# Attention output projection with its weights held in the array, and two edits at the kernel's ends

## What is computed

```
x = x + attention(layernorm(x)) @ Wo      # 16 heads, key width 8, value width 64, causal
x = x + moe(layernorm(x))                 # 8 experts, each takes its top 64 of 256 tokens per batch
                                          # gelu(xin @ w1) @ w2, hidden 512, scaled by the gate's probability
```

## Time and profile before

| | us |
|---|---|
| median of 3 runs | 532.89 |
| the profiled execution | 532.7 |
| its span | 531.0 |
| TensorE busy in the span | 511.3 |
| VectorE, ScalarE, GpSimd busy | 421.9, 397.4, 262.8 |

### The profile page before, as it was taken

The page is one execution under the profiler, slowest core; times in us unless marked ns, Lnnn a source line. Parts: engine busy times, 40 slices in busy tenths (PEclk is TensorE's granted clock), DMA queues, the critical chain, the costliest instruction groups (busy, mean ns, idle before and its releaser), DMA issues.

```text
span 531.0 us, 13930 instructions
## 1 busy us (share of the span) xinstructions
PE 511.3 (96%) x4783; PEld 424.6 (80%) x4783; DVE 421.9 (79%) x1080; ACT 397.4 (75%) x1380; POOL 262.8 (49%) x252
## 2 busy tenths in 40 slices
PE   3799999999999999999999999999999999999996
PEld 2477787787887787787787787877889998999996
DVE  6778889888898898889999999998874677634444
ACT  4799998989889898998989889898654544434330
POOL 8955656556655655656555655665633110011121
PEclk9889999999999999999999999999999999999999
DMA  6575234551622505234151331503200012000002
GB/s 184 174 188 159 79 82 134 185 159 59 183 97 62 158 7 151 79 79 137 24 160 60 102 112 49 160 0 82 81 1 1 2 39 63 22 12 21 11 22 61
DMA packets 48583, 45.70 MB, mean 86 GB/s; under 512 B 3344, under 2 KB 45328, under 8 KB 48528
## 3 DMA queue, kind: packets, MB, share of 16 engines
q1 hardware_dynamic: 47696, 44.33, 28.9%
q10 hardware_dynamic: 832, 0.66, 0.4%
HBM read 26.09 MB, written 18.89 MB: 85 GB/s over the span
## 4 chain that ended last, share of the span: by engine, by line
PE 92%; DVE 2%; ACT 2%; issue 2%; DMA 1%; POOLq 0%; POOL 0%; ACTq 0%
PE ctx_ps L1272 17%; PE misc_ps L1281 11%; PE t_ps L1359 10%; PE t_ps L1245 6%; PE t_ps L1246 5%; PE t_ps L1255 5%; PE misc_ps L1183 4%; PE s_ps L1343 4%; PE misc_ps L1185 4%; PE s_ps L1231 3%; PE misc_ps L1184 3%; PE s_ps L1344 3%; PE s_ps L1345 3%; PE s_ps L1218 3%; PE s_ps L1227 3%; PE ctx_ps L1369 2%
## 5 line engine op out<-in xcount | busy, mean ns | idle before, releaser
L587 ACT ACTIVATE prob<-s_ps,neg_max 128x128 f32<-128x128 f32 (+1 forms) x512 | 209.9, 443 | 0.6 <-DVE neg_max L1100 0.3
L511 POOL TENSOR_TENSOR probn<-prob,inv 128x1024 f32<-128x1024 f32 x64 | 121.2, 1893 | 34.1 <-DVE inv L1080 33.8
L587 ACT ACTIVATION_READ_ACCUMULATOR prob<-s_ps,neg_max 128x1 f32 x512 | 118.1, 231 | 0.0
L504 POOL TENSOR_TENSOR probn<-prob,inv 128x512 f32<-128x512 f32 x64 | 66.6, 1040 | 74.8 <-PE t_ps L1255 74.1
L635 ACT ACTIVATE hT<-s_ps 128x512 f32<-128x512 f32 x64 | 37.9, 597 | 63.4 <-PE s_ps L1345 60.9
L1016 DVE TENSOR_REDUCE neg_max<-s_ps 128x4 f32<-128x1024 f32 x63 | 76.5, 1214 | 5.7 <-PE s_ps L1231 3.5
L1281 PE MATMUL misc_ps<-wo_sb,ctxT 128*128 128x128 f32 x512 | 67.7, 275 | 0.0
L540 POOL TENSOR_TENSOR y_parts<-y_sb,y_parts 128x512 fp32r<-128x512 f32 x16 | 21.2, 1328 | 93.9 <-ACT y_parts L645 93.9
L1281 PEld LDWEIGHTS misc_ps<-wo_sb,ctxT 128*128 128x128 f32 x512 | 62.2, 192 | 0.2 <-issue 0.2
L1245 PE MATMUL t_ps<-ident,probn 128*128 128x128 f32 x256 | 61.7, 281 | 0.0
L1246 PE MATMUL t_ps<-ident,probn 128*128 128x128 f32 x256 | 60.1, 275 | 0.0
(11 more groups left out here) (199 smaller groups left out, 1175.9 us busy)
## 6 DMA issues: line engine op xcount, KB each, us to landing
qT<-q_rows SPq DMA_DIRECT2D x14, 512.0 KB, 4.1
q_rows<-qk_hi SPq DMA_DIRECT2D x16, 256.0 KB, 2.2
q_rows<-qk_lo SPq DMA_DIRECT2D x16, 256.0 KB, 2.7
k_rows<-qk_hi SPq DMA_DIRECT2D x15, 256.0 KB, 2.6
k_rows<-qk_lo SPq DMA_DIRECT2D x15, 256.0 KB, 2.8
k_diag_even<-k_rows SPq DMA_DIRECT2D x28, 128.0 KB, 4.4
k_diag_odd<-k_rows SPq DMA_DIRECT2D x28, 128.0 KB, 4.5
w_raw<-in_L_ffn_w SPq DMA_DIRECT2D x1, 2048.0 KB, 9.3
```

What stands on the lines that cost most here:

```text
L504: nc.gpsimd.tensor_tensor(probn[r][:, 0:HG * P].rearrange("p (i k) -> p i k", i=HG), prob[r][:, 0:HG * P].rearrange("p (i k) -> p i k", i=HG),
L511: nc.gpsimd.tensor_tensor(probn[r][:, HG * P:].rearrange("p (i k) -> p i k", i=HG), prob[r][:, HG * P:].rearrange("p (i k) -> p i k", i=HG ...
L587: last = nc.scalar.activation(prob[r][:, first + i * keys:first + (i + 1) * keys], scores[:, i, :], ACT.Exp, bias=neg_max[:, r, block_, i: ...
```

## The change

Three groups of edits:

**Projection.** In batches 0 to 14 a chunk of Wo (128 x 128) is the stationary operand and the context chunk moves with all its 256 tokens: 2 matmuls a unit. The sum of a batch comes out with tokens along the free axis. ScalarE copies it to `xn2` at the end of unit j = 2 of the next batch (`copy_sums`), TensorE turns it back with two transposes after the contexts of j = 3 (`turn_sums`) into the other half of `misc_ps[1]`, and `add_x` reads it there. Batch 15 keeps the old form.

**Start.** The own keys are made before the own queries, in separate PSUM banks; ScalarE makes the keys' signed copy and writes two of the four key blocks, VectorE the rest by copies. The stores of batch 0 are split: group 1 first (SyncE and ScalarE), the rest on SyncE. GpSimd waits for `own_ready` before wv_lo. Values of unit 1 go to `misc_ps[1]`, so that the values of unit 2 need no copy to be done first; ScalarE's copies of both move from unit 0 to unit 1.

**End.** VectorE makes both parts of the last expert product's result itself (`last_y`, 1 + 4 instructions). TensorE finishes batches 12, 13 and 14 one after the other, and batch 15 in two halves of 128 tokens in banks of their own. VectorE adds these in tiles, and the stores are issued one by one, by SyncE (12, 14, the last half) and ScalarE (13, the first half).

```diff
+        last_halves = [to[:, 0:T].rearrange("p (a d) -> p a d", a=2) for to in (misc_ps[1], s1_ps[:, 0, :])]
...
-        own_ps = misc_ps[1][:, :].rearrange("p (w t) -> p w t", w=2)
+        own_ps = [misc_ps[1][:, 0:T], t_ps[0][:, 0:T]]
...
+                if b == 0:
+                    group, rest = slice(HG, 2 * HG), slice(2 * HG, H)
+                    store_rows(sp, b, qk_hi, K_HI, group, group_stored)
+                    sp.wait_ge(qk_lo_done, b + 1)
+                    store_rows(sp, b, qk_lo, K_LO, group, group_stored)
+                    for source, rows in ((qk_hi, Q_HI), (qk_hi, K_HI), (qk_lo, Q_LO), (qk_lo, K_LO)):
+                        store_rows(sp, b, source, rows, rest)
+                    sp.wait_ge(group_stored, QK_STORES)
+                    sp.wait_ge(zeroed[b], 1)
+                    load_rows(b, slice(1, 2), group_loaded)
+                else:
+                    store_rows(sp, b, qk_hi, Q_HI)
                     store_rows(sp, b, qk_hi, K_HI)
-                sp.wait_ge(qk_lo_done, b + 1)
-                store_rows(sp, b, qk_lo, Q_LO)
-                if b > 0:
+                    sp.wait_ge(qk_lo_done, b + 1)
+                    store_rows(sp, b, qk_lo, Q_LO)
                     store_rows(sp, b, qk_lo, K_LO)
                 sp.wait_ge(qk_stored, QK_STORES * (b + 1))
...
+            for b in range(LAST, B - 1, 2):
+                sp.wait_ge(out_ready, b + 1)
+                sp.dma_start(out_tiles[:, b * TB:(b + 1) * TB, :], x_all[:, b * TB:(b + 1) * TB, :]).then_inc(stored, 16)
+            sp.wait_ge(last_half_ready, 2)
+            sp.dma_start(out_tiles[:, B * TB - 1:, :], x_all[:, B * TB - 1:, :]).then_inc(stored, 16)
+            sp.wait_ge(stored, 16 * (B + 1))
...
+            pool.wait_ge(own_ready, 1)
...
+            def split_own_keys():
+
+                act.wait_ge(own_done, 1)
+                act.wait_ge(signs, 3)
+                nc.scalar.activation(own_hi[:, 1, :], own_ps[1], ACT.Copy, scale=hi_sign[:, 1:2]).then_inc(own_k_hi_done, 1)
+
+            def own_keys():
+
+                act.wait_ge(own_k_done, 1)
+                for i in range(2, HG):
+                    rows = slice(i * ROWS, (i + 1) * ROWS)
+                    last = nc.scalar.activation(k_diag[0][rows, 0, i, :], f32(own_hi[rows, 1, :]), ACT.Copy)
+                last.then_inc(own_keys_ready, 1)
...
+            def copy_sums(b):
+
+                act.wait_ge(wo_done, (b + 1) * G)
+                await_count(act, xg_lo_done, b)
+                await_count(act, x2T_done, b)
+                nc.scalar.activation(xn2[:, :, :].rearrange("p t d -> p (t d)"), misc_ps[1][:, 0:T],
+                                     ACT.Copy).then_inc(sums_copied, 1)
...
+                    if at(u, (1,)):
+                        copy_values(1, 1, 0, misc_ps[1])
...
+                    if at(u, (1,)):
+                        copy_values(2, 2, 0)
+                    if has(u + 2, UNITS) and not at(u, (0,)):
                         copy_values(u + 2, (j + 2) % G, par if j < 2 else 1 - par)
+                    if j == 2 and has(b - 1, B):
+                        copy_sums(b - 1)
...
-            store_rows(act, 0, qk_hi, K_HI)
+            store_rows(act, 0, qk_hi, Q_HI, slice(HG, 2 * HG), group_stored)
+            split_own_keys()
             act.wait_ge(qk_lo_done, 1)
-            store_rows(act, 0, qk_lo, K_LO)
+            store_rows(act, 0, qk_lo, Q_LO, slice(HG, 2 * HG), group_stored)
+            own_keys()
             zero_keys(0, 3, zeroed[0])
+            act.wait_ge(own_keys_ready, 1)
...
+            act.wait_ge(out_ready, LAST + 2)
+            act.dma_start(out_tiles[:, (LAST + 1) * TB:(LAST + 2) * TB, :],
+                          x_all[:, (LAST + 1) * TB:(LAST + 2) * TB, :]).then_inc(stored, 16)
+            act.wait_ge(last_half_ready, 1)
+            act.dma_start(out_tiles[:, B * TB - 2:B * TB - 1, :], x_all[:, B * TB - 2:B * TB - 1, :]).then_inc(stored, 16)
...
-                for w in range(2):
-                    nc.vector.tensor_scalar(own_hi[:, w, :], own_ps[:, w, :], hi_sign[:, w:w + 1], None,
-                                            ALU.mult).then_inc(own_hi_done, 1)
-                dve.wait_ge(own_hi_done, 2)
+                nc.vector.tensor_scalar(own_hi[:, 0, :], own_ps[0], hi_sign[:, 0:1], None, ALU.mult).then_inc(own_q_hi_done, 1)
+                dve.wait_ge(own_k_hi_done, 1)
+                nc.vector.scalar_tensor_tensor(out=own_hi[:, 1, :], in0=own_ps[1], scalar=is_low[:, 1:2],
+                                               in1=f32(own_hi[:, 1, :]), op0=ALU.mult, op1=ALU.add).then_inc(own_k_done, 1)
+                dve.wait_ge(own_q_hi_done, 1)
+                nc.vector.scalar_tensor_tensor(out=qT[0][:, 0, :], in0=own_ps[0], scalar=is_low[:, 0:1],
+                                               in1=f32(own_hi[:, 0, :]), op0=ALU.mult, op1=ALU.add)
+                dve.wait_ge(own_k_done, 1)
                 dve.wait_ge(zeroed_own, 1)
-                nc.vector.scalar_tensor_tensor(out=qT[0][:, 0, :], in0=own_ps[:, 0, :], scalar=is_low[:, 0:1],
-                                               in1=f32(own_hi[:, 0, :]), op0=ALU.mult, op1=ALU.add)
-                for i in range(HG):
+                for i in range(2):
                     rows = slice(i * ROWS, (i + 1) * ROWS)
-                    last = nc.vector.scalar_tensor_tensor(out=k_diag[0][rows, 0, i, :], in0=own_ps[rows, 1, :],
-                                                          scalar=is_low[rows, 1:2], in1=f32(own_hi[rows, 1, :]),
-                                                          op0=ALU.mult, op1=ALU.add)
+                    last = nc.vector.tensor_copy(k_diag[0][rows, 0, i, :], f32(own_hi[rows, 1, :]))
                 last.then_inc(own_ready, 1)
 
...
-                nc.vector.tensor_tensor(x_all[:, tiles, :], misc_ps[1][:, 0:T].rearrange("p (t d) -> p t d", t=TB),
+                if isinstance(b, int) and b == B - 1:
+                    dve.wait_ge(wo_done, B * G)
+                    source = misc_ps[1][:, 0:T]
+                else:
+                    dve.wait_ge(sums_turned, b + 1)
+                    source = misc_ps[1][:, T:2 * T]
+                nc.vector.tensor_tensor(x_all[:, tiles, :], source.rearrange("p (t d) -> p t d", t=TB),
...
+            def last_y():
+
+                dve.wait_ge(y_done, B)
+                chances = slot_prob[:, EP - 1, LAST:B]
+                parts = y_parts[LAST // QB % RING]
+                nc.vector.tensor_tensor(parts[:, :, EP - 1, 0, :], y_ps, bcast(chances, 2, D), ALU.mult).then_inc(last_y_hi, 1)
+                dve.wait_ge(last_y_hi, 1)
+                for q in range(QB):
+                    nc.vector.scalar_tensor_tensor(out=parts[:, q, EP - 1, 1, :], in0=y_ps[:, q, :], scalar=chances[:, q:q + 1],
+                                                   in1=f32(parts[:, q, EP - 1, 0, :]), op0=ALU.mult,
+                                                   op1=ALU.subtract).then_inc(last_y_ready, 1)
+
+            def add_last_half(tb):
+
+                tile = x_all[:, (B - 1) * TB + tb, :]
+                dve.wait_ge(last_half_done, tb + 1)
+                nc.vector.tensor_tensor(tile, last_halves[tb][:, 0, :], tile, ALU.add).then_inc(last_half_added, 1)
+                dve.wait_ge(last_half_added, tb + 1)
...
+                if not (isinstance(w, int) and w >= UNITS - G):
+                    for c in range(2):
+                        last = nc.tensor.matmul(misc_ps[1][:, 0:T], wo_sb[:, 2 * g + c, :], ctxT[r][:, c, :],
+                                                start=(g == 0 and c == 0), stop=(g == G - 1 and c == 1),
+                                                skip_group_check=True)
+                    last.then_inc(wo_done, 1)
+                    return
...
+            def turn_sums(b):
+
+                pe.wait_ge(sums_copied, b + 1)
+                for tb in range(TB):
+                    last = nc.tensor.transpose(misc_ps[1][:, T + tb * P:T + (tb + 1) * P], xn2[:, tb, :], ident[:, :])
+                last.then_inc(sums_turned, 1)
...
+                        pe.wait_ge(v_ready, 1)
+                        values(1, 0, misc_ps[1])
...
+                    if j == 3 and has(b - 1, B):
+                        turn_sums(b - 1)
...
-                        await_count(pe, v_ready, w)
+                        if at(u, (0,)):
+                            pe.wait_ge(qk_lo_done, 2)
+                        else:
+                            await_count(pe, v_ready, w)
...
-            for b in range(LAST, B - 2):
+            for b in range(LAST, B - 1):
                 out_product(b, range(EP - 1))
-            pe.wait_ge(y_lo_ready, B)
-            for b in range(LAST, B - 2):
+                pe.wait_ge(last_y_ready, b - LAST + 1)
                 out_product(b, [EP - 1]).then_inc(out_done, 1)
-            for b in range(B - 2, B):
-                out_product(b, range(EP)).then_inc(out_done, 1)
```

(60 more changed lines are left out.)

9 lines of the change are left out of this document (2 added, 7 removed).

## The result

After the change the kernel takes 534.58 us, median of 20 runs (532.64 to 536.44), beside 532.82 us for the kernel before in 20 runs (531.76 to 534.34) on the same chip. The ratio is 1.0032, interval 1.0022 to 1.0041: the change costs 1.7 us. The profiled execution of after took 536.32 us with a span of 534.6, which is 1.7 us above the median.

A forecast was written before the change was run, and what follows sets the result against it. TensorE's own work was taken to bound the attention loop, with TensorE waiting at start and end. 532.7 + 0.8 - 1.3 - 0.9 = 531.3 us profiled, so 531.5 us; 8-in-10 range 529.2 to 533.9.

The forecast's parts named there:

- Projection: Attention loop: wide records save 1.8 us, transposes add 2.6 us, in all +0.8 us, bounds -0.5 to +4.
- The wide record: Projection on TensorE: a 256-column fp32 record takes 0.215 us, saving 0.03 us a unit over 60 units.
- rival (1): Projection: stationary loads were the limit, so 4 records take 0.47 us and the kernel 508 us; chance 0.08.
- rival (2): Projection: the wide record costs 0.23 us, deciding from 0.222 on, and the kernel takes 535.2 us; chance 0.08.
- A turn: Two transposes behind the contexts of j = 3: +0.17 us for each of 15 batches, +2.6 us.
- The copy on ScalarE: Loop: ScalarE's copy of the sums, 0.41 us, is hidden in its 0.77 us idle time; uncovered, 6 us.
- Rival (5): Loop: the sums' copy is late and TensorE waits, costing as Rival (3) does; chance 0.12 together with Rival (3).
- Start: Start up to unit 2, where the loop is full: -1.3 us, bounds -2.5 to +0.4.
- the split norms: Start, ScalarE: split norms come at 14.5 instead of 15.64, -1.15 us, carried on by scores, maximum and exponentials.
- the values of unit 3: Start, TensorE: these wait for ScalarE's copies of units 1 and 2 and come at about 28.9 instead of 30.4.
- Rival (3): Start: TensorE idles before unit 3's values, the half clock lasts longer, 533.2 us; chance 0.12 together with Rival (5).
- End: From the last product's scaling on: last addition 0.35 us earlier, store queue another 0.55; -0.9 us, bounds -1.5 to +0.2.

The follow-up runs named there:

- e4: The whole change, but GpSimd's `wv_lo` does not wait for `own_ready`; 534.65 us, ratio 1.0047 to the kernel before.
- e7: Kernel before plus all start and end edits, no projection, `wv_lo` held until VectorE's norms of batch 1 are made; 533.24 us, ratio 1.0008.
- e8: Kernel before plus own layout, split stores and end edits, `wv_lo` behind the norms of batch 1, values and projection as before; 530.39 us, ratio 0.9960.
- e10: The whole change with `wv_lo` behind VectorE's norms of batch 1 and the values' edits undone; 531.84 us, ratio 0.9989 to the kernel before.
- e6: Kernel before plus the start's own layout, split stores and `wv_lo` held for `own_ready`, without the values' edits; 532.94 us, ratio 1.0013.
- e3: Kernel before plus the end's edits alone; 531.60 us, ratio 0.9977.
- e1: Kernel before plus the projection's edits alone (wide matmuls, sums copied and turned back); 534.01 us, ratio 1.0027.
- e2: Kernel before plus the start's edits alone (own layout, split stores, `wv_lo` held, values moved); 534.82 us, ratio 1.0044.
- e5: Kernel before plus only the values' edits (unit 1's values in another bank, ScalarE's copies of units 1 and 2 in unit 1); 534.14 us, ratio 1.0033.
- e9: e7 with ScalarE's copies earlier: the first at the end of unit 0, the second behind unit 1's first exponentials; 530.00 us, ratio 0.9958 to before.
- e11: Kernel before plus only the wide projection matmuls, sums added unturned, no copy or transposes (computation partly changed); 531.48 us, ratio 0.9976.

## Why the prediction was wrong

**Projection (forecast +0.8, measured +1.4).** Each mechanism was right. The wide record costs 0.217 us (0.87 for 4), forecast 0.215; the load does not bound it, so rival (1) is out, and rival (2) needed 0.222. A turn costs 0.167 us, forecast 0.17. Two terms of the sum were a little off. The unit gains 0.02 us and not 0.03, because 0.89 - 0.87 was forecast as 0.89 - 0.86: 1.2 us, not 1.8, over 60 units. And the last turn, which is not followed by queries and keys, costs 0.44 us, priced as 0.17. The copy on ScalarE stayed hidden: its busy time in the 340 us rose from 305.67 to 309.78, and TensorE's idle time there went only from 0.82 to 0.98. Rival (5) is out.

The Trainium skill's figure in "TensorE: Matmul & The Clock Gate", section "Back-to-back issue gap", would give 0.109 us for a record with 256 columns at full clock, an estimate by its formula; the 0.217 us measured for fp32 is twice that, and the measurement decides.

**Start (forecast -1.3, measured +2.3).** This is the step that failed, in two places: VectorE's norms were costed at their old length in their new place, and TensorE's wait for ScalarE's copies was taken as gone.

First, "so the split norms come at 14.5 instead of 15.64: -1.15 us". I counted GpSimd's instructions that moved with `wv_lo`, and asked when its own results would be late. I did not ask what VectorE would do beside it. Before, `wv_lo` ran at 11.17 to 13.52 beside VectorE's key blocks, which have PSUM among their sources and were not stretched. The new wait puts it exactly beside two norms whose source is SBUF, 0.60 us of work that became 2.64, and the maximum of the first scores and TensorE's transposes stand behind them. e4, e7 and e8 show it from three sides: with `wv_lo` moved off them the norms take 0.60, and in e4 the copies from SBUF that stand beside it instead are stretched and the instructions with a PSUM source are not. With the wait moved, the split norms come at 14.55 to 15.03 (e7 to e10). Price: e8 against e6 and e3, 0.3%, 1.6 us.

The Trainium skill has this in "SBUF — State Buffer", section "Who interferes with whom": VectorE and GpSimd share one pair of SBUF ports, held for a whole instruction by whoever gets it first, and copies, casts and tensor_scalar contend for it when they run in a mode that uses two ports. Which mode the norms ran in no row here shows. The trace agrees for after: the second norm ends 0.08 us behind `wv_lo`. It does not agree beside GpSimd's next instruction, the zero filling: in e4 the first copy took 1.62 us, until 13.64, with `wv_lo` ending at 13.50, but the second took 1.03 us and did not wait out the filling's 2.82; and in e1 two norms at 14.19 take 0.60 us in the middle of that filling (13.35 to 18.87), as with GpSimd idle. So what stretches the norms is shown for `wv_lo`, and not for GpSimd's work in general.

Second, "the values of unit 3, which wait for both, come at about 28.9 instead of 30.4". They came at 30.89 (29.97 in e2, 30.55 in e7), after 1.90 us of idle time. ScalarE's second copy stands behind the exponentials of unit 1 and the copies of the turned probabilities (29.74, `probT`), and these themselves wait for TensorE. TensorE's wait at 24.85 was not removed, as I had it, but moved to a later place. Rival (3) named the place and the effect, with a chance of 0.12, and priced it at 533.2 us, too little; the sum put it at nothing. e5 (+1.7 us alone) and e9 against e7 (-0.5%, with nothing altered but when two copies run) show the place.

What makes it dear is the half rate, if it falls there. The stretches at 0.50 between 8 and 41 us, and the mark, in every profile (TensorE's wait before the values of unit 3 beside them):

| profile | at 0.50 (us) | wait | mark |
|---|---|---|---|
| after | 23.74 to 27.16, 30.57 to 37.40 | 1.90 | 46.63 |
| e2 | 29.66 to 36.49 | 1.90 | 45.75 |
| e7 | 14.70 to 21.53, 31.77 to 35.18 | 1.90 | 44.93 |
| e4 | 15.18 to 22.01 | 1.91 | 42.98 |
| e5 | 22.71 to 29.53 | 1.26 | 43.23 |
| before | 23.55 to 30.38 | none | 43.12 |
| e1 | 22.98 to 29.81 | none | 42.76 |
| e3 | 15.18 to 28.83 | none | 43.31 |
| e6 | 25.87 to 29.28 | none | 42.49 |
| e8 | 22.86 to 29.69 | none | 42.22 |
| e9 | 23.06 to 26.48 | none | 41.85 |
| e10 | none | none | 42.05 |
| e11 | 15.25 to 18.66, 25.49 to 28.90 | none | 41.84 |

The three with half rate beyond 31 us are late. The ten others are between 41.84 and 43.31, whatever half rate they had earlier: e3 had 13.65 us of it and e10 none. I read this so: until 31 us other engines set the pace, and from there on TensorE does. Take half of the late stretch off the marks of the three (3.4, 3.4 and 1.7 us, an estimate: at 0.50 the work of half the time gets done) and they stand at 43.2, 42.3 and 43.2, among the others. The times point the same way: six executions of after with a mean granted clock of 0.997 took 533.06 to 533.63 us, seven at 0.990 took 534.33 to 536.44; in e10, without the wait, two at 0.987 took 531.48 and 531.93, two at 0.999 took 531.75 and 531.84. So against before the late half rate is most of what such an execution loses; the wait alone leaves the start about even, without the forecast gain. No run held the clock fixed, the records of unprofiled executions don't say where the half rate lay, and what decides whether it comes behind the wait (after) or not (e4) stays open.

**End (forecast -0.9, measured -1.2 in e3).** Right in each step: the four short instructions take 0.28 us each (forecast 0.30), an addition of 128 columns 0.28 to 0.29, the queue's lag 0.03 (forecast 0.07). The profile of after has 1.4 us less from the last scaling on (9.45 - 8.06). The bounds held it.

**Sum.** 1.0044 x 1.0027 x 0.9977 = 1.0048, and the change has 1.0032; the intervals overlap, and e2's own executions differ by 3.4 us (533.27 to 536.69). In microseconds: forecast +0.8 - 1.3 - 0.9 = -1.4; measured parts +1.4 + 2.3 - 1.2 = +2.5; the change +1.7.

## What to carry to other kernels

When an instruction on GpSimd is moved, list what VectorE runs in its new place, with the sources, as well as who waits for its result. When a wait of TensorE's is removed by moving a copy, follow the copy through its own engine's queue to the next reader; idle time that only moves from a stretch with gaps into one without gaps can be a loss, because the clock may fall behind it. Time the parts of a change by themselves: here one lost more than another gained, and one changed wait was worth 0.3%. And do not take a single profile for the median: those of e4, e5 and e6 were the fastest of their sets, and the same start gave marks 1.5 us apart.

## What the runs showed of the hardware

- VectorE beside one GpSimd tensor_tensor of 128x1024 (2.35 to 2.45 us): two tensor_scalar of 128x128 from SBUF took 2.64 us instead of 0.60, two copies of 32x256 from SBUF 2.66 instead of 0.57; an instruction with a PSUM source kept its 0.47. Beside GpSimd's zero filling (2.8 us each, a broadcast source) two norms took 0.60 in e1, as alone.
- GpSimd's own instruction lost little: 2.45 us beside the norms in after, 2.35 without them in e4, e7 and e8.
- A full-width fp32 record of 256 columns takes 0.217 us, two of 128 columns 0.222.
- Idle time of 1.90 us on TensorE was followed by a stretch at the 1.2 GHz level in after and e2 (6.83 us long) and in e7 (3.41 us), and not in the profiled e4 (1.91 us idle), nor in e5 after 1.26 us.
- Half rate before 31 us moved the start of unit 2's contexts by no more than it spreads anyway (43.31 in e3 after 13.65 us of it, 42.22 in e8 after 6.83, 42.05 in e10 with none); half rate beyond 31 us went with 44.93 to 46.63 (e7, e2, after).
